# A three-layer Perceiver block on one core: who loads x, who spreads the biases, and when a bias row is added to x

## The reference

```
LN(x): (x - mean) / sqrt(var + 1e-5)
x = x + xattn(LN(x), ctx)   q = LN(x)Wq + bq; k = ctx Wk + bk; v = ctx Wv + bv
                            softmax(q k' / 16) v, then Wo, + bo
x = x + attn(LN(x))         causal self-attention inside each batch of 64 tokens
x = x + ffn(LN(x))          LN(x) + 2 shared experts + top 2 of 8 routed experts
                            (each: 256 -> 1024, gelu, 1024 -> 256)
```

## Time and profile before

| | us |
|---|---|
| median of 3 runs | 253.06 |
| lowest and highest | 252.71, 253.97 |
| the profiled execution, whole | 252.87 |
| its span, first to last instruction | 251.1 |
| TensorE busy | 242.7 (97% of the span) |
| VectorE busy | 153.5 (61%) |
| ScalarE busy | 135.5 (54%) |
| GpSimd busy | 50.2 (20%) |

### The profile page before, as it was taken

The page is one execution under the profiler, slowest core; times in us unless marked ns, Lnnn a source line. Parts: engine busy times, 40 slices in busy tenths (PEclk is TensorE's granted clock), DMA queues, the critical chain, the costliest instruction groups (busy, mean ns, idle before and its releaser), DMA issues.

```text
span 251.1 us, 5120 instructions
## 1 busy us (share of the span) xinstructions
PE 242.7 (97%) x1908; PEld 209.4 (83%) x1908; DVE 153.5 (61%) x371; ACT 135.5 (54%) x265; POOL 50.2 (20%) x81
## 2 busy tenths in 40 slices
PE   8799998999999999999999999999999999999994
PEld 8656645366367599999998999999999999999994
DVE  0833244453654897788849246666667666667683
ACT  2225205152152778886867256666666666666641
POOL 5100000000100200230587002112122111126700
PEclk9999999999999999999999999999999999999999
DMA  7999999999999999950157448999999999920142
GB/s 253 423 432 397 423 407 431 377 404 425 356 379 341 323 315 426 422 238 0 45 169 295 105 130 287 364 373 364 360 354 349 371 346 360 347 117 21 54 137 84
DMA packets 14254, 74.12 MB, mean 295 GB/s; under 512 B 1524, under 2 KB 8956, under 8 KB 9884
## 3 DMA queue, kind: packets, MB, share of 16 engines
q1 hardware_dynamic: 12700, 70.59, 74.9%
q0 software_dynamic: 1008, 2.76, 2.9%
q10 hardware_dynamic: 528, 0.52, 0.6%
HBM read 67.56 MB, written 6.32 MB: 294 GB/s over the span
## 4 chain that ended last, share of the span: by engine, by line
PE 71%; DMA 15%; DVE 4%; POOL 3%; issue 2%; SPq 2%; ACT 2%; DVEq 0%; POOLq 0%; ACTq 0%
PE psum L512 61%; DMA rows<-rows_dram 11%; PE psum L760 4%; POOL slot_x_dram L479 3%; DMA slot_x_dram<-second,rows_of 3%; PE psum L601 2%; PE psum L778 1%; DMA xrow<-slot_x_dram 1%; ACT prob L879 1%; DVE cmax L1083 1%; PE psum L821 1%; SPq L337 1%; PE psum L650 1%; PE psum L692 0%; DVE xs L1107 0%
## 5 line engine op out<-in xcount | busy, mean ns | idle before, releaser
L512 PE MATMUL psum<-xrowT,ring 128*128 128x128 f32 x480 | 58.3, 275 | 0.0
L512 PEld LDWEIGHTS psum<-xrowT,ring 128*128 128x128 f32 x480 | 56.2, 192 | 0.0
L1303 DVE TENSOR_TENSOR dlo<-ring,dhi 128x1024 fp32r<-128x1024 f32 x30 | 38.3, 1280 | 3.8 <-ACT dhi L962 3.8
L1322 DVE TENSOR_TENSOR slot_hlo<-slot_h,slot_hhi 128x512 fp32r<-128x512 f32 x30 | 20.8, 693 | 30.0 <-ACT slot_hhi L990 30.0
L988 ACT ACTIVATE slot_h<-psum 128x512 f32<-128x512 f32 x30 | 18.0, 600 | 35.5 <-PE psum L512 35.5
L512 PE MATMUL psum<-dhi,slot_hhi 128*128 128x256 f32 x120 | 36.3, 302 | 0.1
L512 PE MATMUL psum<-dhi,slot_hlo 128*128 128x256 f32 x120 | 33.8, 282 | 0.0
L512 PE MATMUL psum<-dlo,slot_hhi 128*128 128x256 f32 x120 | 33.8, 282 | 0.0
L962 ACT ACTIVATE dhi<-ring 128x1024 fp32r<-128x1024 f32 x30 | 31.1, 1040 | 0.0
L504 POOL DMA_INDIRECT results_dram<-y_rows,result_row x13 | 14.6, 1119 | 72.6 <-DMA results_dram<-y_rows,result_row 56.2
L512 PE MATMUL psum<-xh,parted 128*128 128x256 f32 x128 | 26.8, 286 | 0.0
(11 more groups left out here) (195 smaller groups left out, 398.4 us busy)
## 6 DMA issues: line engine op xcount, KB each, us to landing
ring<-experts_dram SPq DMA_DIRECT2D x15, 2048.0 KB, 8.5
ctx<-ctx_dram SPq DMA_DIRECT2D x4, 3072.0 KB, 24.5
ctxT_start<-ctxT_start_dram SPq DMA_DIRECT2D x4, 2048.0 KB, 19.0
ctxT_rest<-ctxT_rest_dram SPq DMA_DIRECT2D x4, 1154.0 KB, 21.4
raw<-experts_dram SPq DMA_DIRECT2D x2, 2048.0 KB, 15.4
slot_x_dram<-empty_row SPq DMA_DIRECT2D x1, 1935.0 KB, 16.2
xrow<-slot_x_dram SPq DMA_DIRECT2D x15, 129.0 KB, 7.4
squares<-squares_dram SPq DMA_DIRECT2D x1, 1285.0 KB, 14.2
```

Source lines behind the costliest of these rows:

```text
L512: return pe.matmul(out, lhsT, rhs, start=first, stop=last)
L1303: dve.tensor_tensor(dlo[b % 2][:, steps, :], ring[b][:, steps, C * P:STEP_W], dhi[b % 2][:, steps, :].bitcast(F32), ALU.subtract).then_inc ...
L1322: dve.tensor_tensor(slot_hlo[:, half, :], slot_h[:, half, :], slot_hhi[:, half, :].bitcast(F32), ALU.subtract).then_inc(slot_hlo_ready, 1)
```

## The change

There are four edits.

1. x is loaded by the first transfer on SyncE's queue, and its array in memory is laid out on the host as it will lie on chip (128 partitions, each with its 4 x 256 numbers in one stretch).
2. `squares[:, 0:2]` is loaded from ScalarE's queue instead.
3. The six products that spread the bias columns are done by ScalarE, as the first instructions after its transfer; on VectorE two of them stood between the statistics and the normalisation of x and four behind the dot products of x.
4. Adding the bias row to x becomes an item of the list of its own, ("x_bias",), which stands behind the four `exp` items of pair 1 and ahead of the last piece of W of pair 0. The row is kept in `v2` and no longer in `mix`.

```diff
-                  ("exp", t + 1, 2), ("exp", t + 1, 3), ("W", t, 3 if t else 4, KT)]
+                  ("exp", t + 1, 2), ("exp", t + 1, 3), *([] if t else [("x_bias", )]), ("W", t, 3 if t else 4, KT)]
...
         def _(sp):
-            sp.dma_start(squares[:, 0:2], squares_d[:, 0:2]).then_inc(query_squares_in, 16)
+            sp.dma_start(xs[:, :, :], x_d).then_inc(x_in, 16)
             sp.dma_start(cols[:, :, :], cols_d.rearrange("(c p) n -> p c n", p=P)).then_inc(cols_in, 16)
...
         def _(act):
-            act.dma_start(xs[:, :, :], x_d.rearrange("(t p) d -> p t d", p=P)).then_inc(x_in, 16)
+            act.dma_start(squares[:, 0:2], squares_d[:, 0:2]).then_inc(query_squares_in, 16)
+            act.wait_ge(consts, 7)
+            act.wait_ge(cols_in, 16)
+            for n, col in enumerate((XBK, XBV, ABK)):
+                for c in range(C):
+                    ins = act.activation(bcast[:, n, c, :], ones[:, :], ACT.Copy, scale=cols[:, c, col:col + 1])
+                ins.then_inc(bcast_ready, 1)
...
             dve.wait_ge(consts, 7)
-            dve.wait_ge(cols_in, 16)
-
-            def spread(n, col):
-                for c in range(C):
-                    ins = dve.tensor_scalar(bcast[:, n, c, :], ones[:, :], cols[:, c, col:col + 1], None, ALU.mult)
-                ins.then_inc(bcast_ready, 1)
-
-            spread(0, XBK)
             dve.wait_ge(rstd_ready, 1)
...
-            spread(1, XBV)
-            spread(2, ABK)
...
-            dve.tensor_copy(mix[:, :], bank(PO, 0, D)).then_inc(fold_dve, 1)
+            dve.tensor_copy(v2[:, :], bank(PO, 0, D)).then_inc(fold_dve, 1)
...
+            def x_bias():
                 dve.wait_ge(fold_dve, 2)
                 dve.wait_ge(rows_in, 16)
-                link(dve.tensor_tensor(mix[:, :], mix[:, :], rows[:, 0:D], ALU.add))
+                link(dve.tensor_tensor(v2[:, :], v2[:, :], rows[:, 0:D], ALU.add))
                 for t in range(T):
-                    ins = dve.tensor_tensor(xs[:, t, :], xs[:, t, :], mix[:, :], ALU.add)
+                    ins = dve.tensor_tensor(xs[:, t, :], xs[:, t, :], v2[:, :], ALU.add)
                 link(ins)
...
-        "x_in_dram": a["x"].reshape(N, D),
+        "x_in_dram": a["x"].reshape(T, P, D).transpose(1, 0, 2),
```

More of the change, by code:

```diff
@@ L1304, in split_down @@
                                   dhi[b % 2][:, steps, :].bitcast(F32), ALU.subtract).then_inc(dlo_ready, 1)
-            mine = {"T": probT_copy, "bias_folds": bias_folds, "S": max_chunk, "W": weigh, "mixT": mixT_copy, "proj": x1_stats,
+            mine = {"T": probT_copy, "bias_folds": bias_folds, "x_bias": x_bias, "S": max_chunk, "W": weigh, "mixT": mixT_copy, "proj": x1_stats,
                     "norm2": norm2, "norm3": norm3,
```

## The result

| | before | after |
|---|---|---|
| median of 11 runs, us | 252.95 | 251.74 |
| lowest and highest | 252.47, 253.97 | 251.36, 252.25 |
| the profiled execution, whole | 252.87 | 252.07 |
| its span | 251.1 | 250.3 |
| VectorE busy | 153.5 | 152.4 |

The ratio is 0.9953 (95% interval 0.994 to 0.9965): 1.2 us less, against a forecast of 251.8 from a median of 253.06. The size agrees. The rows are from the timeline of the changed kernel (start, length, engine, line of that kernel, what, idle before).

A forecast was written before the change was run, and what follows sets the result against it. It took VectorE's wait for rows, leaving TensorE idle 1.17 us before pair 1's transposes, as the bound. Terms: -1.17 (idle hidden) - 0.2 (start) + 0.2 (given back at raw) = -1.2 us, giving 251.8; range 251.1 to 253.0.

The forecast's parts named there:

- Moving the bias row: At pair 1's transposes: exponentials start at 37.90 instead of 39.19 and are hidden by 0.13 us; -1.17 us.
- The start: First loads: x lands about 4.8 us, squares about 5.8, transposes at 9.65; about 0.2 us gained.
- The spreads: Six spreads on ScalarE: 1.6 us in all, first two done by 7.2, all by 8.3; no gain taken.
- The gate at raw: Around 84 us: TensorE, ahead by 1.4 us, waits for the norm behind raw's first split; 0.2 us given back.
- x's larger packets: First transfers: x's larger packets save 0.17 us, so raw lands that much earlier too.
- My own sign of being wrong: Listed signs: fold after 6.3 us, TensorE waiting over 0.3 us for pair 1's context, or 1.4 us ahead at 90 us.
- first rival: At raw: the gate does not hold, saving 1.4 to 1.7 us or a little more; 251.3 us, chance 0.20.
- The squares were not starved: Rival, first loads: squares wait behind context rows, landing at 10 us; slower kernel, 255.9 us, chance 0.09.
- The start did not lose: Rival, first loads: squares land at 6.3 us or later, transposes 0.3 to 0.8 late; 252.4 us, chance 0.15.
- the additions are not in the way: Rival, VectorE: moved additions hold up pair 0's scaling, TensorE loses its gain at mixT; 252.9 us, chance 0.06.

The follow-up runs named there:

- e1: Kernel before with only the bias row moved (edit 4), loads and spreads as before; 252.12 us, ratio 0.9946.
- e11: Kernel before with only the bias row moved, run again on the same chip as the whole change; 251.81 us, ratio 0.9935.
- e6: Changed kernel with its first two transfers exchanged: squares from SyncE's queue, x in 4 KB rows from ScalarE's; 252.23 us, ratio 0.9947.
- e7: Changed kernel with raw made late by four blocks of slot-buffer zeros put ahead of it in SyncE's queue; 252.30 us, ratio 0.9954.
- third group: Four kernels (e10, e11, e12, e13) run on one chip beside the kernel before, whose median there was 253.12 us.
- e12: The whole change, unaltered, run again as reference for the other three of its group; 251.62 us, ratio 0.9929.
- e10: Kernel before with only the bias row moved and the first split of raw put behind the two norms; 251.78 us, ratio 0.9947.
- e13: Whole change with the first split of raw put behind the two norms, run again; 251.27 us, ratio 0.993.
- e8: Changed kernel with raw made late as in e7 and the first split of raw behind the two norms; 251.52 us, ratio 0.9929.
- e9: Changed kernel, unaltered, run again on the same chip as e7 and e8; 251.42 us, ratio 0.9932.
- e2: Changed kernel with the bias row back in its old place, so only loads and spreads change; 252.79 us, ratio 0.998.
- e3: Changed kernel with the first split of raw put behind the two norms; 252.06 us, ratio 0.9957.

## Why the prediction was right, and where it was not

**Moving the bias row: right.** Forecast 1.17 us of idle time hidden with a margin of 0.13 and exponentials after 6.86 us; measured none left, 6.81 us, and TensorE 1.42 us ahead against 1.4 with the start. That this alone carries the change, within what can be told, is shown by e1 and e11.

**The start: the sum was right by luck, its step was not.** "x then arrives at about 4.8 instead of 5.9" failed: it arrives at 5.8 in the first profile. I had read the 4.0 and 5.2 us of the earlier trace rows as places in a line, which an exchange swaps. They went with how x was laid out, in rows of 1 KB, as e6 shows. The forecast had `xn` ready at 8.1, a full microsecond ahead of need, and TensorE, held by the squares, as what sets the transposes. Measured, `xn` starts at 9.14 and sets them itself, by its 0.56 us; TensorE alone, 0.95 us behind the start of its bias product at 8.66 as in e7, could have begun at 9.61. So 9.70 against the forecast 9.65 is two paths that happen to end 0.1 us apart, and most of what was won is that x landed 0.15 us earlier (5.79 against 5.94). Over all profiles the first scores of pair 0 start at 15.00 to 15.10 us with the old start in four executions and 14.88 in the fifth, and at 14.80 to 15.11 in eight with the new one (e6 apart); the means are 15.02 and 14.92. So the start is worth 0.1 us in these profiles and not 0.2, less than one execution varies. The medians of the third group point to 0.2 to 0.5 (e11 against e12, e10 against e13), within their noise.

**The spreads: cost nothing, by luck of cover.** The six took 1.86 us, 0.31 each, against 0.27 from the earlier trace rows. The table load of 1.28 us, which came only after `cols`, was not in my account at all. It had 0.5 us of cover left: the first two spreads end at 8.1, and TensorE comes at 8.66.

**The gate at raw: right as a mechanism, wrong as a constant.** The forecast for TensorE's load was 83.93 and the first profile has 83.94, so this step could not have come out closer; e7 and e8 show that it is the path. But I gave `raw` one landing time, less 0.17 us for x's larger packets. That 0.17 did not come (81.86 against 81.79), and between executions of one kernel it lands between 80.8 and 81.9 us. An execution that is not held has its transpose at about 83.5 and so bears a `raw` up to 2.06 us ahead of that, 81.5; the landings lie on both sides of it. In two of three profiles of the change nothing was held. My own sign of being wrong, TensorE ahead by 1.4 us or more at 90 us, is there in both: its product `mixT` of pair 3 starts at 90.01 us in the kernel before, at 89.00 in the first profile, and at 88.49 (e9) and 88.57 (e12), 1.5 and 1.4 us ahead. So my forecast and its first rival (the gate does not hold) are each true in some executions, though not for the reason that I gave for the rival, which was less work ahead of `raw`. How often the gate is paid is not shown. The median of 1.2 us less is the smallest of the three measurements of the change (1.2, 2.0 and 1.5 us), and the last two are no smaller than the 1.4 us that TensorE won; the intervals overlap, but the close agreement of the first with -1.2 may well be in part luck.

**The rivals.** The squares were not starved: 5.2 us from ScalarE's queue, with context rows behind x in SyncE's. The Trainium skill (DMA: Bandwidth & Descriptors, Queues, rings and completion order) has an engine drain a whole packet of one queue before it turns to the next. The delay that I had let follow from this, with several context rows in one turn ahead of the squares, is not in any run here: they landed 5.1 to 5.4 us after issue in all eight profiles in which they came from ScalarE's queue. The start did not lose, and the additions are not in the way (VectorE waits 0.59 us after them).

**Small terms not seen.** The 0.2 us at the routed rows in the first profile looks like variation between executions: the wait of TensorE's product there was 0.42 us in it, 0.21 in the kernel before and none in e9 and e12. What makes it vary was not looked for.

## What to carry to other kernels

When a stall is removed, look down the path of the engine that gets ahead for the next landing with less slack (time between landing and need) than the gain, and for what stands in front of the awaited instruction in its engine's program: here two norms behind a split whose data came late. Take that slack from several executions before it is called a limit, since transfers land up to a microsecond apart from run to run. And before two transfers are exchanged between queues, compare the lengths of their rows, since an early landing may belong to the shape of the transfer beside it and not to its place.

## What the runs showed of the hardware that I had not expected

Two transfers of half a megabyte issued together landed 3.8 to 4.0 and 5.0 to 5.2 us after issue when one had rows of 4 KB and the other of 1 KB, and within 0.3 us of each other, at 4.9 to 5.5 us, when both had rows of 4 KB (after, e2, e3, e6, e7, e8, e9, e12, e13). The later of the two landed no sooner. A table load on ScalarE can move with the code: it ran at 1.27 us before, although the first arithmetic instruction behind it waited for TensorE until 6.87, and at 6.23 us, when `cols` had landed, once the first arithmetic instruction waited for GpSimd's constants and for `cols`. Why the one wait did not hold it and the other did was not tested.
